# Order of beta, mean and seed for the pairs whose second batch ScalarE seeds

## What is computed

```
h       = relu(x[b] @ W1[id] + b1[id])
y       = x[b] + h @ W2[id] + b2[id]
normed  = (y - mean(y)) * rsqrt(var(y) + 1e-5)        # over the 512 of a row
out[b]  = x[b] + normed * gamma[id] + beta[id]
```

## Time and profile before

| what | value |
|---|---|
| median of 3 runs | 329.36 us (328.43 to 332.5) |
| profiled execution | 329.88 us, its span 328.1 us |
| granted TensorE clock, mean over the span | 0.969 |
| busy: TensorE, VectorE, ScalarE, GpSimd | 298.1, 307.4, 235.8, 186.8 us |
| from 100 to 300 us: TensorE, VectorE, ScalarE, GpSimd | 197.4, 198.3, 151.8, 119.5 us of 200 |
| from 100 to 300 us: clock, DMA traffic | 1.00, 347 GB/s |

### The profile page before, as it was taken

How to read it: one execution, slowest core, us unless ns; L and a number is a source line. 1 busy time by engine, 2 the same in 40 slices (tenths; PEclk the granted TensorE clock), 3 DMA queues, 4 the chain that set the end, 5 groups by cost and what they waited for, 6 DMA issues and landing times. The chain is left out here.

```text
span 328.1 us, 7357 instructions
## 1 busy us (share of the span) xinstructions
PE 298.1 (91%) x2008; PEld 257.1 (78%) x2039; DVE 307.4 (94%) x621; ACT 235.8 (72%) x543; POOL 186.8 (57%) x217
## 2 busy tenths in 40 slices
PE   2766779999999999999999999999999999999962
PEld 2246678888888888888888888888888888888941
DVE  5699828999999999999999999999999999999996
ACT  3976517877777777778787777777778787777762
POOL 2952614566555666555566555566655566555563
PEclk9879859999999999999999999999999999999998
DMA  5999999999999999999999999999999999999924
GB/s 155 345 401 345 299 343 382 357 332 352 342 341 360 335 343 338 352 336 337 354 338 362 347 343 321 373 364 347 344 336 348 357 352 323 377 322 372 353 102 185
DMA packets 64792, 109.22 MB, mean 333 GB/s; under 512 B 4315, under 2 KB 15639, under 8 KB 64625
## 3 DMA queue, kind: packets, MB, share of 16 engines
q1 hardware_dynamic: 64654, 108.62, 96.4%
q10 hardware_dynamic: 99, 0.14, 0.1%
HBM read 44.78 MB, written 33.55 MB: 239 GB/s over the span
## 5 line engine op out<-in xcount | busy, mean ns | idle before, releaser
L346 POOL TENSOR_TENSOR x_io<-x_io,beta_all 128x512 f32<-128x512 f32 x128 | 162.2, 1288 | 0.2 <-issue 0.2
L471 PE MATMUL ps_h<-x_T,w_stage 128*128 128x128 f32 x1024 | 127.3, 278 | 0.0
L471 PEld LDWEIGHTS ps_h<-x_T,w_stage 128*128 128x128 f32 x1024 | 121.9, 195 | 0.8
L403 ACT ACTIVATE cut<-ps_y,row_sum 128x512 bf16<-128x512 f32 x128 | 88.0, 687 | 40.8 <-PE ps_y L492 38.0
L643 DVE SCALAR_TENSOR_TENSOR x_io<-ps_y,rstd,x_io 128x512 f32<-128x512 f32 x128 | 90.2, 746 | 2.3
L630 DVE SCALAR_TENSOR_TENSOR ps_y<-ps_y,neg_mean,gamma_all 128x512 f32<-128x512 f32 x128 | 90.0, 746 | 2.0 <-ACT cut L403 2.0
L341 POOL TENSOR_TENSOR neg_mean<-row_sum,neg_over_h 128x2 f32<-128x2 f32 x64 | 12.8, 200 | 128.9 <-ACT ps_y L413 75.0
L611 DVE SCALAR_TENSOR_TENSOR ps_y<-x_io,b_all 128x512 f32<-128x512 f32 x93 | 85.2, 941 | 0.0
L457 PE MATMUL ps_T<-identity,x_io 128*128 128x128 f32 x512 | 69.1, 280 | 11.9 <-DMA x_io<-in_x 10.2
L457 PEld LDWEIGHTS ps_T<-identity,x_io 128*128 128x128 f32 x512 | 61.9, 144 | 21.0 <-issue 12.8
L492 PE MATMUL ps_y<-w_high,h_high 128*128 x128 | 62.9, 492 | 8.4 <-DVE h_low L598 3.1
(11 more groups left out here) (66 smaller groups left out, 130.5 us busy)
## 6 DMA issues: line engine op xcount, KB each, us to landing
x_io<-in_x SPq DMA_DIRECT2D x64, 512.0 KB, 5.7
out<-x_io SPq DMA_DIRECT2D x63, 512.0 KB, 4.7
w_stage<-w_all SPq DMA_DIRECT2D x116, 256.0 KB, 3.5
w_stage<-in_L_cond_W SPq DMA_DIRECT2D x12, 256.0 KB, 6.4
x_io<-in_L_cond_W SPq DMA_DIRECT2D x5, 512.0 KB, 8.1
b_all<-in_L_cond_b SPq DMA_DIRECT2D x1, 2560.0 KB, 13.9
w_all<-in_L_cond_W SPq DMA_DIRECT2D x5, 512.0 KB, 7.5
out<-x_io SPq DMA_DIRECT2D x2, 256.0 KB, 2.0
```

What stands on the lines that cost most here:

```text
L346: nc.gpsimd.tensor_tensor(x_slot(t), x_slot(t), of_lang(beta_all, lang), ALU.add).then_inc(x_beta_ready, 1)
L403: nc.scalar.activation(squares[:, t % 2, :], ps_y[t % Y_BANKS][:, :], ACT.Square, scale=-float(H), bias=stat(row_sum, t), accum_out=stat(s ...
L471: last = nc.tensor.matmul(bank[:, b * S:(b + 1) * S], w1_stage[:, 2 * (p % STAGE_PAIRS) + b, c, :], x_T[:, (2 * p + b) % 4, c, :], start=F ...
```

## The change

In GpSimd's program, for the pairs whose second batch ScalarE seeds: wait for VectorE's seed of the first batch, add beta of the first batch, then the mean (which waits for both seeds), then beta of the second batch. The other pairs keep their order.

In ScalarE's program: the seed of batch 2k + 3 is issued ahead of square_pair(k), no longer between copy_x and high_h; the same in the last pairs.

```diff
             for n in range(PAIRS):
                 langs = langs_of(pool, n)
-                mean_of_pair(n)
-                for b in range(2):
-                    add_beta(2 * n + b, langs[b])
+                if by_scalar(2 * n + 1):
+                    wait_seed(pool, 2 * n)
+                    add_beta(2 * n, langs[0])
+                    mean_of_pair(n)
+                    add_beta(2 * n + 1, langs[1])
+                else:
+                    mean_of_pair(n)
+                    for b in range(2):
+                        add_beta(2 * n + b, langs[b])
...
                 if p < PAIRS - 1:
                     copy_x(p + 1)
-                t = 2 * (p - FIRST) + 3
-                if by_scalar(t):
-                    seed(t)
                 high_h(p)
...
             for p in range(FIRST, PAIRS):
+                t = 2 * (p - FIRST) + 3
+                if by_scalar(t):
+                    seed(t)
                 square_pair(p - FIRST)
                 step(p)
             for n in range(PAIRS - FIRST, PAIRS):
-                square_pair(n)
                 if n + 1 < PAIRS and by_scalar(2 * n + 3):
                     seed(2 * n + 3)
+                square_pair(n)
```

## The result

| | before | after |
|---|---|---|
| median | 330.43 us (4 runs) | 338.44 us (4 runs, 336.94 to 339.28) |
| profiled execution, its span | 329.88, 328.1 us | 338.47, 336.5 us |

The ratio is 1.024, with an interval of [1.016, 1.032]: slower, by 8.0 us of the medians and 8.6 of the profiled executions; the interval leaves open whether it is by more than 2%. I had forecast some 20.8. (In what follows medians take in all executions of a kernel, ratios only the undisturbed ones, so the two can differ by 1%.)

The account below looks back on a forecast made before the run. VectorE was taken to bound the kernel, TensorE close behind. Stalls of 1.46 us per period less 0.72 for the collision took the period from 8.92 to 9.66 us: 43.5 - 22.7 = +20.8 us, so 350 us, range 335 to 361.

Parts of the forecast that it names:

- the chain finish, seed, square: ScalarE's seed waits for VectorE's finish, the squares queue behind it, and VectorE's scaling stalls 0.88 us per period.
- the register load behind it: VectorE's load of language ids starts only after the late second scaling, delaying the reciprocal by 0.55 us per period.
- Part 1, the collision: GpSimd's new order stops its beta addition from holding up VectorE's seed: 0.72 us less per period, 22.7 us in all.
- rival D: GpSimd's additions slide onto another VectorE seed, leaving the stalls alone: +43 us, 373 us, chance 0.05.
- Part 2, the stall: ScalarE's seed ahead of the squares makes VectorE's scaling wait 0.88 us per period, the second scaling 0.03 more.
- a sign that it is wrong: The prediction is wrong if VectorE's reciprocal follows the scalings at once, or squares still end ahead of the scaling.
- The sum: Stalls of 1.46 us per period less 0.72 lengthen VectorE's period from 8.92 to 9.66 us; +20.8 us overall.
- rival A: The forecast itself with bounds on hand-overs and VectorE's exposed register load: 340 to 363 us, chance 0.75.
- rival B: VectorE stalls but its register load hides, as transfers get more room: 335 us, partial exposure up to 340, chance 0.13.
- TensorE close behind, at 8.57: TensorE waits 0.35 us per period for low_h and could run at 8.57 us, next behind VectorE.
- rival C: ScalarE's seed finds its bank free, the collision goes, TensorE bounds at 8.57 us: 319 us, chance 0.07.
- Others that the delay reaches: ScalarE's copy_x runs from about 5.4 to 6.4 us; TensorE may wait 0.2 to 0.5, covered by the longer period.

Follow-up runs that it names:

- e4: Kernel before, with GpSimd's additions of beta over only 2 of the 512 columns: 328.7 us, ratio 0.996.
- e2: Kernel before with ScalarE's new order alone, GpSimd's order as before: median 341.8 us, ratio 1.025.
- e1: Kernel before with GpSimd's new order alone, ScalarE's seed where it was: 328.5 us, ratio 0.995.
- e9: Changed kernel with half of each W1 copy left out from pair 4 on: 333.2 us, ratio 1.010.
- e11: Changed kernel with SyncE waiting for the store of one pair earlier (p - 2, not p - 1): 341.3 us, ratio 1.035.
- e13: Changed kernel with SyncE's order store, W1, W1, x in place of W1, W1, store, x, its register load ahead of the store: 347.3 us, ratio 1.050.
- e5: e1 with half of each W1 copy left out from pair 4 on: 317.0 us, ratio 0.958.
- e8: e1 with ScalarE's seed placed between the squares and copy_x: 327.5 us, ratio 0.992.
- e7: e1 with SyncE reading the language ids of two pairs in one register load: 322.1 us, ratio 0.975.
- e12: Changed kernel with VectorE reading two pairs' ids in one register load, behind scalings that don't wait for a square: median 337.1 us, ratio 1.021.

## Why the prediction was off

Direction and place were right, and so was the main mechanism, the chain finish, seed, square. The size was not: the term of **the register load behind it**, 0.55 us per period, is the step that failed. It measured 0.19.

- *Part 1, the collision* (-0.72 us per period): the size held. The part of the period from scale(n+1) on, where no load shows, fell from 5.15 to 4.43, and e4 shows that the collision was the cause. But the prediction booked this as the gain of GpSimd's order. By e2 the stall alone brings it, and GpSimd's order alone (e1) brings only 8.2 of the 22.3 us. The sum doesn't suffer, since the collision goes once and was counted once. But the price of the stalls alone, 373 us (rival D), is wrong for this reason: e2, which has nothing but the stalls, has 341.8. That the moved addition costs nothing under low_h and scaling held nearly: 420 against 416 ns, 752 against 746.
- *Part 2, the stall* (0.88 + 0.03): 0.83 measured (4.60 against 3.77). Hand-over 0.09 for my 0.15, seed to square 0.63 for 0.60, square to sum 0.76 for 0.77, sum to scaling 0.20 for 0.22; the 0.03 for the second scaling didn't show. An excess of 0.08 x 29 = 2.3 us. The wait stayed at 23 to 25 us in e9, e11 and e13, whatever the transfers did: it is a chain between two engines.
- *The register load* (0.55): 0.19 measured, the mean of 4.62 against 4.43. An excess of 0.36 x 29 = 10.4 us, most of the miss. That it shows at all, and only when it is longer than some 0.66 us, was right. (The idle time in the rows is 0.09 us less than what a load costs, since a reciprocal that doesn't wait starts 0.09 before the scalings end.) But it mostly isn't: in 18 of the 29 iterations the reciprocal follows the scalings at once, which the prediction had named as a sign that it is wrong. I gave the load the median of all of VectorE's loads before. In its new place, over 29 iterations, its mean is 0.78 us, while the loads of the odd iterations (5 to 61) have 1.46. One from each place:

```profile
...
L171 DVEq TENSOR_LOAD <-lang_ids x1: 528/528/528, 125.5 to 125.5; - x1
```

```profile
...
L171 DVEq TENSOR_LOAD <-lang_ids x1: 1200/1200/1200, 128.4 to 128.4; - x1
```

The group of reciprocals over the whole run:

```profile
...
L641 DVE RECIPROCAL rstd<-std 128x2 f32<-128x2 f32 x64 | 10.1, 158 | 4.5 <-issue 4.4
```

e9 (fewer bytes: 0.58), e11 (0.92) and e13 (the burst moved onto it: 1.18) show that the mean length in one and the same place of VectorE's program follows the traffic around it. Why it is short in the new place is argued, not shown: the stall ties VectorE's load to finish, and finish also releases the store, so the load falls mostly between two bursts of issues, in 22 of the 29 iterations 1.2 to 2.5 us after the issue of x's load started. Which part of the traffic counts stays open. In four iterations in a row (loads at 145.05 to 172.16) a copy of W1 was issued only 0.05 to 0.60 us ahead of the load, and it took 0.52 to 0.55 us all the same. The lowest row was in truth nearer than the median. The floor of 600 ns in the Trainium skill (DMA: Bandwidth & Descriptors, Latency and other measured facts), taken as typical, would have been too low by 0.2 here, and by 0.9 for the loads of the odd iterations; the shortest here, 0.52 us, lie under it.
- *The sum*: per period 0.83 + 0.19 - 0.73 = 0.29, x 29 = 8.5 us, as in the trace. The forecast had 0.74.
- *The rivals*: 338.4 us lies inside the range of 335 to 361, but outside the bounds of the forecast itself (rival A, 340 to 363, chance 0.75). It is rival B with a partial exposure, 335 to 340, which had 0.13. B's reason is not borne out, though. It had the longer period leave the transfers more room, yet the loads of the odd iterations grew from a mean of 1.14 us to 1.46; only those in the new place shrank, from 1.30 to 0.78.
- *TensorE close behind, at 8.57* (rival C's price, 319): the floor was right (e5), but rival C's time was not. Between VectorE and TensorE stands SyncE's chain, at 8.9 (e1, e4). The prediction saw TensorE wait for nothing but low_h and has no term for SyncE. Before the change SyncE waited for VectorE's finish only 5.1 us in the 200 from 100 to 300 us, so it had next to no slack, and a seed that finds its bank free brings what e8 has, 2.6 us, not 11. For the forecast itself this didn't matter, since the new period is above 8.9: in the changed kernel SyncE waits for finish 14.2 us of the 200, and TensorE never waits for W1 there.
- *Others that the delay reaches*: copy_x ran from 125.63 to 126.62, 5.3 to 6.3 into the period. TensorE waits for it some 0.4 us per period (8.0 us, 21 times, from 100 to 300 us), within the forecast of 0.2 to 0.5, and it doesn't set the pace. Rival D (373) is out: no seed is slow.

## What to carry to other kernels

Moving an instruction ahead in an in-order engine moves its wait too. Before doing it, look when the thing waited for comes (here 2.3 us after ScalarE is free) and what is queued behind it. If a sequencer loads registers behind such a wait, cost the load at the place in the traffic where it will then lie. And before taking a busy engine's lost time for gain, take it away in a run of its own (e4): an engine without idle time can sit just above another chain that is nearly as long. Two parts of a change are also better priced in runs of their own (e1, e2) than added up.

## What was not expected of the hardware

- The granted clock was 1.00 from 100 to 300 us in both kernels, so the difference between them is not the clock's.
- From 100 to 300 us the transfer engines show a busy share of 1.00 to 1.01 at 345 to 348 GB/s (before, after, e1), and 1.00 at 359 (e7): here a share of 1.00 was no ceiling.
- A register load of two ids from SBUF takes between 0.5 and 2.3 us. How much it loads doesn't settle its length: the loads of four ids on SyncE in e7 (22 from 100 to 300 us) had a mean of 0.8 us, where those of two before had 1.5, but those on VectorE in e12 had 2.2, where those of two in the same iterations of the changed kernel had 1.46.
